# A chain of four layers on one core: composed projections, layer one inside the attention loop, cached blocks in units of 128, scores in row tiles

## The reference

```python
x = x + einsum('bct,bcd->bdt', x, W0[cond])                      # a 32x32 mix per sequence
x = x + x @ W.T + ((x @ A[i].T) @ Bm[i].T) * s[i]                # layer 1: shared W, adapter i per sequence, rank 16
x = x + attention(x)                                             # layer 2, below
x = x + x @ W3[id] + b3[id]                                      # layer 3: one of 16 experts per sequence
```

## Time and profile before

| | |
|---|---|
| median of 3 runs | 190.97 us (190.74 to 191.12) |
| profiled execution, its own span from first to last instruction | 198.3 us |
| PE busy | 127.1 us (64%) |
| weight loads | 95.6 us (48%) |
| DVE busy | 109.9 us (55%) |
| ACT busy | 85.4 us (43%) |
| POOL busy | 79.4 us (40%) |
| DMA | 31.70 MB, mean 160 GB/s |

### The profile page before, as it was taken

How to read it: one execution, slowest core, us unless ns; L and a number is a source line. 1 busy time by engine, 2 the same in 40 slices (tenths; PEclk the granted TensorE clock), 3 DMA queues, 4 the chain that set the end, 5 groups by cost and what they waited for, 6 DMA issues and landing times.

```text
span 198.3 us, 3786 instructions
## 1 busy us (share of the span) xinstructions
PE 127.1 (64%) x1182; PEld 95.6 (48%) x1182; DVE 109.9 (55%) x404; ACT 85.4 (43%) x274; POOL 79.4 (40%) x105
## 2 busy tenths in 40 slices
PE   0224999600796940003672899498795989899983
PEld 0114855300655830001572776386674768677652
DVE  0877662002998779700716886355555585878211
ACT  0300300039634479500336498344556484855310
POOL 3378432100043200077762988672747731314000
PEclk9999999965599995555566579759999999999999
DMA  4969999998577766878640322311656736365661
GB/s 116 271 132 213 223 175 188 208 165 216 141 183 207 190 169 172 272 217 254 206 116 27 79 79 79 83 53 55 204 171 164 222 105 178 93 191 155 190 186 46
DMA packets 33535, 31.70 MB, mean 160 GB/s; under 512 B 6636, under 2 KB 31340, under 8 KB 32812
## 3 DMA queue, kind: packets, MB, share of 16 engines
q1 hardware_dynamic: 27090, 19.46, 34.9%
q0 software_dynamic: 3216, 11.15, 24.7%
q10 hardware_dynamic: 3210, 0.87, 2.2%
HBM read 23.47 MB, written 8.00 MB: 159 GB/s over the span
## 4 chain that ended last, share of the span: by engine, by line
PE 32%; DMA 21%; DVE 12%; issue 12%; ACT 8%; SPq 7%; another core or an unknown queue 4%; POOL 3%; DVEq 0%; ACTq 0%
DMA blk<-in_L_cond_k_blocks,tab_i 12%; PE bank L1080 7%; SPq L341 7%; DMA kv_rows<-blk 6%; PE bank L1097 5%; PE bank L1127 5%; PE bank L1140 4%; PE bank L1114 3%; ACT QBD L562 3%; PE bank L1135 3%; DMA lens_i<-in_itok_B 2%; DVE S L898 2%; ACT PTA L577 2%; POOL tab_i L393 2%
## 5 line engine op out<-in xcount | busy, mean ns | idle before, releaser
L1080 PE MATMUL bank<-KT,QBD 128*128 128x160 f32 x128 | 29.7, 368 | 7.5 <-ACT QBD L562 5.0
L589 ACT ACTIVATE pr<-S,nb 128x160 f32<-128x160 f32 x64 | 26.9, 423 | 11.1 <-DVE nb L898 5.2
L1080 PEld LDWEIGHTS bank<-KT,QBD 128*128 128x128 f32 x128 | 22.9, 231 | 12.3 <-issue 9.9
L889 DVE TENSOR_SCALAR pr<-pr,ri 128x128 f32<-128x128 f32 x64 | 22.8, 413 | 1.1
L898 DVE CUSTOM_DVE_ANT_0 S<-bank,mask 128x160 f32<-128x160 f32 x64 | 17.9, 316 | 6.4 <-PE bank L1080 4.1
L874 DVE COPY KT<-bank 128x512 f32<-128x512 f32 x8 | 5.5, 690 | 26.7 <-issue 11.3
L460 POOL TENSOR_TENSOR prB<-pr,ri 128x64 f32<-128x64 f32 x32 | 9.5, 296 | 25.3 <-DVE ri L885 25.1
L1011 PE MATMUL bank<-WkvT,x2T 128*128 128x256 f32 x32 | 9.4, 458 | 14.5 <-DVE WqT L768 12.8
L1060 PE MATMUL bank<-cst,kvA 128*128 128x128 f32 x16 | 4.6, 395 | 20.7 <-DMA kvA<-kv_rows,rowA 20.7
L434 POOL DMA_INDIRECT kvA<-kv_rows,rowA x16 | 15.9, 997 | 4.5 <-issue 4.5
L577 ACT COPY PTA<-bank 128x256 f32<-128x256 f32 x32 | 11.9, 372 | 12.8 <-PE bank L1097 12.7
(11 more groups left out here) (182 smaller groups left out, 284.4 us busy)
## 6 DMA issues: line engine op xcount, KB each, us to landing
We<-in_L_cond_W SPq DMA_DIRECT2D x16, 256.0 KB
kvn<-in_L_cond_W SPq DMA_DIRECT2D x16, 256.0 KB
kv_rows<-blkp SPq DMA_DIRECT2D x2, 968.0 KB
xin<-in_x SPq DMA_DIRECT2D x2, 512.0 KB
kv_rows<-kvn SPq DMA_DIRECT2D x2, 512.0 KB, 7.3
be<-in_L_cond_b SPq DMA_DIRECT2D x32, 32.0 KB
out<-nat SPq DMA_DIRECT2D x8, 128.0 KB
kv_rows<-QBD SPq DMA_DIRECT2D x1, 968.0 KB
```

What stands on the lines that cost most here:

```text
L589: act.activation(pr[:, n // B4 % 2, u, n % B4, :], S[:, n % 2, u, :], ACT.Exp, bias=nb[:, n % 4, u:u + 1], scale=-1.0, accum_out=rs[:, n % ...
L889: ts(e_, e_, ri[:, n % 8, u:u + 1], None, ALU.mult).then_inc(s_pn, 1)
L1080: i_ = mm(bank[3 + n % 2][:, u * KEYS:(u + 1) * KEYS], QBD[:, g % 2, j, 2 * u:2 * u + 2, :].rearrange("p g c -> p (g c)"), KT[:, g % 2, j, :],
```

## The change

- **Mix.** No way through DRAM: DVE turns the gathered matrices by one 32-by-32 transpose, DVE and ACT copy the parts into `mix`, which POOL has zeroed.
- **Units.** The 352 window blocks are numbered through and cut into three units of 128 partitions. ACT does all permutations; keys and values of a unit land in one `window` buffer and are written by one DMA in pieces of 16 KB (unit 2 by four of 4 KB pieces). Unit 2's values are loaded only after the first eight gathers, permuted in step 4 of the loop, and written ahead of the expert loads. A gather waits only for the units that it reads.
- **Composed weights.** With W + I in `nat`, PE forms (W + I)^T Wk^T and so on and the same for the adapter's up matrix, so K, V and Q come from x1T and xaT in three calls per tile of rows.
- **Layer 1 in the loop.** Its four pieces run at steps -1, 1, 3 and 6; ACT keeps them.
- **Queries in quarters.** The first is rotated before the loop, the others by DVE in steps 1 to 10; PE turns them at steps 4, 10, 14, and ACT keeps them in `QT`, plain, not block-diagonal.
- **Scores in row tiles.** Four calls per sequence with 32 rows and 64 columns of weights each.
- **Other moves.** Keys are kept by ACT, not DVE; distances and masks of groups 2 to 7 are made in the loop; positions and window middles on POOL.

```diff
-UNITS = [(0, 11), (11, 11), (22, 10)]
+NU = 3
+FLAT = B * WB
...
-NROWS = WIN0 + B * WROWS
+NROWS = WIN0 + NU * P * BLOCK
...
 AHEAD = 10
+FIRST = 8
+X2_STEP = (1, 3, 6)
...
-        blk_src = [blk[:, 0, :], blk[:, 1, :], blk[:, 2, :], over_kvA[:, 0, :], over_kvA[:, 1, :],
-                   kvn[:, :, :].rearrange("p n c -> p (n c)")]
-        blk_dst = [blkp[:, 0, :], blkp[:, 1, :], QBD[:, :, :, :, :].rearrange("p i b g c -> p (i b g c)"),
-                   We_own[:, :, :, :].rearrange("p e c o -> p (e c o)"), blk[:, 2, :], over_kvA[:, 0, :]]
+        flat = lambda t: t.rearrange("p i c -> p (i c)")
+        blk_src = [blk[:, 0, :], blk[:, 1, :], blk[:, 2, :], over_kvA[:, 1, :],
+                   flat(QT[:, :, :, :].rearrange("p n b c -> p n (b c)")), flat(We_own[:, :, :, :].rearrange("p e c o -> p e (c o)"))]
+        window = [flat(blkp[:, :, :]), flat(blk[:, 0:2, :]), flat(blkp[:, :, :])]
...
+        UNIT_OF = [(b * WB + WB - 1) // P for b in range(B)]
+        Q_BANK, Q_STEP = (5, 6, 1, 1), (4, 10, 14)
...
-            sp.wait_ge(s_mixg, 16)
-            sp.dma_start(mix_rows.rearrange("(b c) d -> b (c d)", c=T), mixg).then_inc(s_mixs, 16)
-            sp.wait_ge(s_mixs, 16)
-            sp.dma_start(mixw[:, :, :], mix_rows.rearrange("(n p) d -> p n d", p=P)).then_inc(s_mixw, 16)
...
-            for i in (2, 0, 3, 4, 1, 5):
-                u, kv = LOADS[i]
-                b0, nb_ = UNITS[u]
-                n = nb_ * WB
-                sp.wait_ge(s_perm[i], 1)
-                r0 = WIN0 + b0 * WROWS
-                dst = kv_rows[r0:r0 + n * BLOCK, kv * KV:(kv + 1) * KV].rearrange("(p o) c -> p o c", o=BLOCK)
-                sp.dma_start(dst, blk_dst[i][0:n, :].rearrange("p (o c) -> p o c", o=BLOCK)).then_inc(s_winw[i], 16)
+
+            def write_window(u, parts):
+
+                for kv in range(2):
+                    sp.wait_ge(s_perm[2 * u + kv], 1)
+                r0 = WIN0 + u * P * BLOCK
+                dst = kv_rows[r0:r0 + P * BLOCK, :].rearrange("(p o) c -> p (o c)", o=BLOCK)
+                w = BLOCK * 2 * KV // parts
+                for q in range(parts):
+                    sp.dma_start(dst[:, q * w:(q + 1) * w], window[u][:, q * w:(q + 1) * w]).then_inc(s_winw[u], 16)
+
+            write_window(0, 1)
+            write_window(1, 1)
...
             for h in range(2):
                 sp.wait_ge(s_kready, h + 1)
                 r0 = NEW0 + 4 * h * P
                 sp.dma_start(kv_rows[r0:r0 + 4 * P, :].rearrange("(j p) c -> p j c", p=P),
                              kvn[:, 4 * h:4 * h + 4, :]).then_inc(s_neww, 16)
-
+            for b in range(FIRST):
+                sp.wait_ge(s_kvA[b], 16)
+            write_window(2, 4)
...
+            def load_blocks(i):
+                u, kv = LOADS[i]
+                pool.wait_ge(s_tab[u], 16)
+                pool.indirect_dma_start(out=blk_src[i], out_offset=None, in_=(pool_k, pool_v)[kv],
+                                        in_offset=bass.IndirectOffsetOnAxis(ap=tab_i[:, u:u + 1], axis=0)).then_inc(s_bl[i], 16)
+
+            for i in range(5):
+                load_blocks(i)
...
             def gather_b(g):
-                pool.indirect_dma_start(out=kvB(g, slice(0, 2 * KV)), out_offset=None, in_=kv_rows,
+                if g == NT // 2:
+                    pool.wait_ge(s_ss, 6)
+                windows(B4 * g + B4 - 1)
+                pool.indirect_dma_start(out=kvB(g, slice(0, 2 * KV)), out_offset=None, in_=written(B4 * g + B4 - 1),
...
             def gather_a(b):
                 if b % B4 == 0:
                     gather_b(b // B4)
-                pool.indirect_dma_start(out=kvA(b, slice(0, 2 * KV)), out_offset=None, in_=kv_rows,
+                if b == B // 4:
+                    pool.wait_ge(s_perm[3], 1)
+                if b == B // 2:
+                    pool.wait_ge(s_winw[2], 64)
+                windows(b)
+                pool.indirect_dma_start(out=kvA(b, slice(0, 2 * KV)), out_offset=None, in_=written(b),
                                         in_offset=bass.IndirectOffsetOnAxis(ap=rowA[:, b:b + 1], axis=0)).then_inc(s_kvA[b], 16)
...
-            pool.wait_ge(s_l0, 4)
             pool.wait_ge(s_rowi, 5)
-            for i in range(6):
-                pool.wait_ge(s_winw[i], 16)
             pool.wait_ge(s_neww, 32)
-            for b in range(AHEAD):
+            for b in range(FIRST):
                 gather_a(b)
-            pool.wait_ge(s_cst0, 16)
+            load_blocks(5)
...
+            def permute(i):
+
                 src, dst = permutation(i)
                 act.wait_ge(s_bl[i], 16)
+                if i == 2:
+                    for j in range(2):
+                        act.wait_ge(s_perm[j], 1)
+                if i == 4:
+                    act.wait_ge(s_winw[0], 16)
                 act.copy(dst, src).then_inc(s_perm[i], 1)
...
+            def keep_x2(k):
+                act.wait_ge(s_l1, k + 1)
+                act.copy(x2T[:, k % 2, 512 * (k // 2):512 * (k // 2) + 512], bank[(0, 7)[k % 2]][:, :]).then_inc(s_x2, 1)
...
+            def keep_ka(g):
+
+                act.wait_ge(s_kt, 2 * g + 1)
+                if g >= 2:
+                    act.wait_ge(s_sc, 2 * B4 * (g - 1))
+                act.copy(KT[:, g % 2, :, 0:P], bank[1][:, :].rearrange("p (b r) -> p b r", b=B4)).then_inc(s_kta, 1)
+
+            def keep_kb(g):
 
                 act.wait_ge(s_kt, 2 * g + 2)
                 if g >= 2:
-                    act.wait_ge(s_sc, B4 * (g - 1))
-                act.copy(KT[:, g % 2, :, P:KEYS], bank[2][:, 0:P].rearrange("p (b r) -> p b r", b=B4)).then_inc(s_ktb, 1)
...
+                if n == 0:
+                    keep_x2(0)
+                if n in X2_STEP:
+                    keep_x2(1 + X2_STEP.index(n))
+                if n == LAST_UNIT:
+                    permute(5)
                 if n % B4 == 1 and n // B4 + 1 < NT:
-                    keep_q(n // B4 + 1)
+                    keep_ka(n // B4 + 1)
+                if n % B4 == 2 and n // B4 + 1 < NT:
+                    keep_kb(n // B4 + 1)
+                if n in Q_STEP:
+                    keep_q(1 + Q_STEP.index(n))
+                g = n // B4 + 2
+                if g < NT:
+                    if g >= 4 and n % B4 == 0:
+                        act.wait_ge(s_mask, g - 1)
+                    distance(g, n % B4)
...
+            Q_PARTS = {1: (6, 7), 2: (8, 9), **{3 + k: (10 + k,) for k in range(1, 5)}, **{7 + k: (15 + k,) for k in range(1, 5)}}
...
+            dve.wait_ge(s_mixg, 16)
+            step(ts(mixg[:, 0:T * T:T + 1], mixg[:, 0:T * T:T + 1], 1.0, None, ALU.add))
+            dve.transpose(xaT[0:T, :], mixg.rearrange("b (c d) -> b d c", c=T)).then_inc(s_mixt, 1)
...
+            def compose(j, at, src):
+
+                for dc in range(KC):
+                    for oc in range(KC):
+                        mm(bank[j][:, dc * D:(dc + 1) * D], nat[:, oc, 0, dc * P:(dc + 1) * P], src(oc),
+                           start=(oc == 0), stop=(oc == KC - 1))
+                for oc in range(KC):
+                    i_ = mm(bank[at][:, 0:D], natB[:, oc, :], src(oc), start=(oc == 0), stop=(oc == KC - 1))
+                i_.then_inc(s_wt, 1)
...
+            def layer1(k):
+                oc, h = k % 2, k // 2
+                if k == 0:
+                    pe.wait_ge(s_wtA, 10)
+                if k < 2:
+                    pe.wait_ge(s_qk, NT)
+                else:
+                    pe.wait_ge(s_x2, k - 1)
+                o = bank[(0, 7)[k % 2]]
+                for kc in range(KC):
+                    mm(o[:, :], W1T[:, kc, oc * P:(oc + 1) * P], x1T[:, kc, 512 * h:512 * h + 512], start=(kc == 0), stop=False)
+                mm(o[:, :], BT[:, oc * P:(oc + 1) * P], xaT[:, 512 * h:512 * h + 512], start=False, stop=True).then_inc(s_l1, 1)
...
+                    o = bank[1 + i][:, (t % 2) * D:(t % 2) * D + D]
+                    for kc in range(KC):
+                        mm(o, x1T[:, kc, t * P:(t + 1) * P], WkvT[:, kc, :], start=(kc == 0), stop=False)
+                    i_ = mm(o, xaT[:, t * P:(t + 1) * P], BKV[:, :], start=False, stop=True)
+                i_.then_inc(s_kvp, 1)
...
             def scores(n):
+
                 g, j = divmod(n, B4)
                 if j == 0:
                     pe.wait_ge(s_kta, g + 1)
                     pe.wait_ge(s_ktb, g + 1)
-                    pe.wait_ge(s_qt, G * (g + 1))
-                if n >= 2:
-                    pe.wait_ge(s_mx, 2 * (n - 1))
+                    pe.wait_ge(s_qt, g + 1)
                 for u in range(2):
-                    i_ = mm(bank[3 + n % 2][:, u * KEYS:(u + 1) * KEYS],
-                            QBD[:, g % 2, j, 2 * u:2 * u + 2, :].rearrange("p g c -> p (g c)"), KT[:, g % 2, j, :],
-                            start=True, stop=True)
-                i_.then_inc(s_sc, 1)
+                    i = 2 * n + u
+                    if i >= 3:
+                        pe.wait_ge(s_mx, i - 2)
```

(36 more changed lines are left out.)

735 lines of the change are left out of this document (369 added, 366 removed).

## The result

The changed kernel takes 159.76 us (median of 4 runs, 158.55 to 160.91), the kernel before beside it 190.86 (189.22 to 191.12): ratio 0.839, 95% interval 0.833 to 0.846. The runs of one kernel spread by up to 4%; where it matters, the median of those within 1.5% of the kernel's fastest run is given too, as its fast median. The profiled execution is the one of 158.55 us, and its span is 156.7. From that pair, a span is some 1.9 us less than its execution's time, so the profiled execution of before (span 198.3) was some 9 us longer than the median, not the 7.3 that the prediction took.

The account below looks back on a forecast made before the run. The prologue was taken as bound by bytes, then by SP's issue of 512-byte pieces; in the loop PE nearly bounds. 190.97 - 15.0 (prologue) + 5.2 (layer 1) - 2.4 (scores) - 2.8 (QBD copies) = 176.0 us, range 164 to 188.

Parts of the forecast that it names:

- at the 199 GB/s of the loading stage the other 10.35 MB take 52 us: Prologue: bytes left after 15 us land near 67 us, so window gathers start at 69.5 instead of 84.5, 15.0 us earlier.
- the floor: Prologue: if bytes go fast, computing on ACT and the new keys let the gathers start no earlier than 64 us.
- Sum: Whole kernel: 190.97 - 15.0 + 5.2 - 2.4 - 2.8 = 176.0 us.
- 12.4 us from gather to scores: Between first gather and first scores: taken unchanged from the kernel before, so the loop starts at 82 us.
- Layer 1, +5.2: Loop: four pieces, 10.8 us on PE, less 5.6 us of PE idle time; bounds 0 and +20.
- rival of the half clock: Loop: layer 1 runs at half clock, 20 us less 5.6 idle: +9, so 185 us; chance 0.08.
- Scores in 0.55 us: Loop: a sequence's eight score matmuls run two at a time, 0.55 us instead of 1.10 one after another.
- Scores -2.4 and QBD -2.8: Loop: scores save 0.10 us in 24 sequences; dropping QBD copies removes PE's 0.70 us gap in four groups.
- Rotations and masks in the loop, 0, up to 3: Loop, DVE: about 0.7 us per step fits under the step's time; costs nothing, up to +3 us.
- Third unit late: Loop: the third unit's late load and write delay step 10; +10 with 17 us of flight, so 186 us; chance 0.15.
- The loop: Loop length near 99 us, first two groups longer than 16.7 us, steady ones under 11.2.
- Bytes flow faster: Rival for the prologue: gathers at 64 us, scores partly four at a time, 165.5 us; chance 0.15.

Follow-up runs that it names:

- experiments 1 and 2: Kernel before with block loads widened to 128 partitions: 185.03 us against 201.93; changed kernel with loads cut to 121 or 112: 185.65 and 177.63 us against 200.56.
- experiment 2: Changed kernel with block loads cut to 121 or 112 partitions, the rest filled by small DMAs: 185.65 and 177.63 us, kernel before 200.56.
- experiment 4: Changed kernel, one chip (before 202.59 us): unedited 175.37 us; without layer 1 170.80; score calls on all 128 rows 175.24; layer 1's first piece earlier 173.99.
- experiment 5: Changed kernel unedited 160.30 us; third unit loaded early 161.14; without later query rotations 158.32; layer 1's first piece earlier and exponential table loaded later 154.72.
- the base: The changed kernel itself, run again beside its edited versions: 175.37 us where before took 202.59, 160.30 where before took 191.96.

## Why the prediction was wrong

**What failed is one term of the sum: "at the 199 GB/s of the loading stage the other 10.35 MB take 52 us".** The bytes were right: 10.5 MB were moved from 15 us to the first gather. The rate was not. I counted the 0.38 MB that 128 rows add and carried the rate of loads with 121 and 110 rows over to them. Share 0.99 seemed to say that the engines could do no more. It said that they were occupied: by experiments 1 and 2 a packet of 8 KB occupies an engine for about 0.32 us with 128 partitions, 0.50 with 112 and 0.66 with 121. (Busy share of the software queue x 16 engines x window over its packets of 8 KB; for the first, 0.996 x 16 x 10 us / 501.) The gathers came at 48.1 us, not 69.5. Of these 21.4 us experiment 2 gives 11.1 to the loads' width; the rest is in part that window writes ran well above 199 GB/s too, in part open.

The second step that failed is the floor, "if they go fast, 64 us". Bytes did go fast and computing did set the gathers, as that branch said, but at 48.1: the floor stood on load 3 landing at 47.5 us, which is the same slow rate once more. It landed at 29.6 (17.92 and 11.7 of flight), and the new keys were ready at 44.5 us instead of 61.

The Trainium skill has a page on it that I did not weigh. DMA: Bandwidth & Descriptors, The descriptor swizzle, says that in a 1 MiB transfer to 128 partitions each engine writes one port of SBUF. No run here shows ports, but the order 128, 112, 121 fits with engines that get in each other's way once a transfer is cut otherwise. The same page's count of engines (section Why a DMA increments its semaphore by 16 and not by 1: the largest k up to 16 that divides the partitions, so 11 for 121 and 16 for 112) would have warned me too, but it does not explain the rows by itself: share 1.04 with 121 doesn't look like idle engines, and 112 was not as fast as 128. Its 341 GB/s for 1 MB (section Measured), which the prediction had beside the sum, was nearer to the 421 found than my 199.

Point by point, the rest:

- *Sum.* With the gathers at 48.1 instead of 69.5 the prediction's own terms give 154.6. Measured 159.8, so 5.2 us went the other way in what follows. (The prediction's 74 and 57.6 us for other rates also lack the 2.5 us that its 69.5 has.)
- *12.4 us from gather to scores*: 11.0. Right, for another reason: the queries' chain on ACT ends it.
- *Layer 1, +5.2*: taking it out gave 4.6 us in one batch, 4.1 in another, which is near, but with a lower clock in what stayed (experiment 4), so the agreement may be luck. The price also stood on 5.6 us in which PE was idle in before's first groups, and these were not the kernel's own: 2.97 of them are one stretch in which PE, DVE and ACT all stand still, a wait like those in the last section:

```profile
102.92:105.89 2.97, 0.00 (x0) 0.00 (x0) 0.01 (x1) 0.00 (x0) 0.45 (x1) 1.00 0.25 80
```

  The rival of the half clock had the right mechanism for the first piece alone (5.4 against 2.7 us).
- *Scores in 0.55 us*: 0.50 for eight, 0.44 to the next. Two at a time was too few. The Trainium skill's rule (TensorEngine Tiling (Array Packing), Gotcha 1) keeps two row tiles from one bank at the same time. I took it to mean one by one; but a sequence's two pairs write two banks, so it would still allow two at a time. Experiment 4 has 0.70 us for two at a time, and 0.44 is not what the rule gives, though no run isolates one bank.
- *Scores -2.4 and QBD -2.8*: a late group got 1.2 us shorter, where the two were priced at 0.4 and 0.7 for it; that scores of 0.70 us cost nothing that could be told (experiment 4) suggests that it was the gap and not the scores. The QBD copies were not put back alone.
- *Rotations and masks in the loop, 0, up to 3*: 2.0 us for the rotations, 3.8 by fast medians.
- *Third unit late*: POOL waited 4.0 us, and the earlier load gave nothing. The rival as priced is out.
- *The loop*: about 99 us was forecast with "its first two groups longer"; from 59.16 us to the end of the span it is 97.5. But measured against the sum's own 94.0 (176.0 - 82) the time has 100.6 (159.8 - 59.2), 6.6 more. The early steps are the likely place, once they came so soon after the queries: the order of ACT's table and of layer 1's first piece was worth 5.6 us there (experiment 5), on the one chip where it was seen. This price was missing because I had the queries "hidden with 6 us to spare", which the early gathers used up.
- *Bytes flow faster*, the rival with 0.15: the right side, and too small by 6 us for the same reason, since its best rate was 243 GB/s.

The split of the gain is not a plain sum. Width alone gave 12 to 17 us in the kernel before, where SP's issue then bound it, and cost 12 us when taken from the changed one; the remaining 14 to 19 us of the 31.1 are the change's other parts together. These are differences taken on other chips than the 31.1. What makes the engines slower at 112 and 121 partitions is argued, not shown.

## What to carry to other kernels

A DMA share near 1 is occupation, not a rate: divide it by the packets and compare the time of one packet with that of another shape before calling a stage bound by bytes. And don't carry one stage's GB/s over to other transfers: here writes in 16 KB pieces ran faster than the loads that they were priced by. Ask of each edit whether it changes the shape of a transfer (here 121 to 128 partitions, 6% more bytes in half the time), and price that first. When a prologue shrinks, look at once for what is next in line: here a table load ahead of the first keys and one matmul block behind the first scores, 5.6 us for a few moved lines. And look in a trace that runs long for stretches in which every engine stands still, before taking an idle time in it for free room.

## What the runs showed of the hardware

- Block loads of 8 KB per partition by the software queue: 421 to 422 GB/s with 128 partitions, 249 to 283 with 112, 202 to 208 with 121, at a share of 0.99 to 1.06 each time.
- More than two small matmuls can overlap: eight of 160 columns take 0.44 us in four row groups and two column halves, 0.70 us in two column halves with all rows.
- After an idle stretch PE's matmuls of layer 1 ran at the granted clock of 0.50 (5.4 us for a piece), and with PE kept busy at 1.00 (2.6 us).
- On four of the chips the kernel before took 9 to 11 us more, and the changed one 15 us on the one where both ran, with waits like these (timeline of DVE and of ACT, the base on such a chip), whose releaser the profile doesn't know ("remote"). PE's last matmul that either needs ends at 70.8 us:

```profile
72.70 0.33 DVE L940 CUSTOM_DVE_ANT_0 S<-bank,mask 128x160 f32<-128x160 f32 x1 [7.15 <-remote]
```

```profile
71.96 0.58 ACT L618 COPY x2T<-bank 128x512 f32<-128x512 f32 x1 [5.44 <-remote]
```

The cause stays open. The trace of before holds such waits too, which fits its long span.
- A DVE addition of 0.42 us took 1.85 us (70.35) while POOL multiplied 128x512 elements beside it (70.85, 1.05 us), and a DVE scaling whose median is 0.32 took 1.86 (in the pair at 92.44) beside such an operation at 93.35. The base of experiment 5 has the same two, 1.85 and 1.86. Nothing here isolates that.
